# Cross-attention and expert feed-forward kernel: transposing the softmax probabilities with VectorE blocks and a round trip through DRAM instead of on TensorE

## The chip, the cores and the metric

One core of one Trainium2 chip runs the whole program. The metric is the device time of one execution in microseconds (us). TensorE is called PE, VectorE DVE, ScalarE ACT, GpSimd POOL and SyncE, which only issues transfers, SP.

## The reference

`x` and `ctx` are 128 batches of 64 rows by 128 features, float32. One layer of cross attention (16 heads of 64) and one expert feed-forward, each with a residual:

```python
x = x + xattn(ctx, layernorm(x), mask, ...)
    # kv_in = concat(norm(features), norm(latents))   128 rows: 64 of ctx, 64 of x
    # sim   = (lat @ Wq) (kv_in @ Wk)^T * scale, masked; alphas = softmax(sim)
    # out   = (alphas @ (kv_in @ Wv)) @ Wo
x = x + ffn(layernorm(x), ...)
    # 8 experts of width 64, the best 2 per row weighted by a sigmoid gate, and one shared expert of 128
```

## The kernel before

The weights are folded first: `MV[0]` holds Wq Wk^T per head and `MV[1]` Wv Wo per head, so that scores are (lat MV[0]) kv_in^T and the attention's result is the sum over heads of (alphas kv_in) MV[1]. Work goes in **frames**, `i` counts them: one frame is a group of 4 batches (`GB`), and there are 32 groups (`NG`). A frame has 8 steps, `k` = 0 to 7, and `e = 8 * i + k` numbers the steps of the program. In a step one **half** enters: 8 heads of one batch, that is four pairs of heads (`PAIRS`), 128 by 128 scores each. There are 256 halves.

A half `c` goes through these stages, each written in the step given here:

- PE, L858: four score products, float32, into PSUM bank `S_ps` (step c)
- DVE, L654: mask added and maximum taken, `logits` (step c+1)
- ACT, L531: four exponentials with their sums, `probs`, `denom` (step c+1)
- DVE, L662: `rdenom`, and POOL, L430: `probs` times `rdenom` (step c+2)
- PE, L838: four transposes of 128 by 128 by a product with the identity, into PSUM bank `PT_ps`; ACT, L504: `pT_hi`, the rounded high part; DVE, L687: `pT_lo`, what is left (step c+3)
- PE, L796 to L798 (`matmul3`): three products of high and low parts of `kv_in` and `pT` into `C_ps`; ACT, L510: `cT_hi`; DVE, L697: `cT_lo` (step c+4)

`MV[1]` is applied to `cT` of a whole group in the next frame, `W_ps`, heads spread over steps 0 to 5. Beside these stages each frame norms the keys of the group two frames on (POOL, with statistics by DVE at L738 and L743), transposes them (PE, L872), projects the queries of the next group (two heads a step, `T_ps`, copied by ACT to `tT`), adds the residual and takes statistics (DVE, L707 to L716), computes the gate (DVE, L579 to L617), and runs the feed-forward of the group before (PE into `H_ps`, ACT `h_tanh`, DVE `h_silu` and `h`, POOL `h` times `gates`, PE `Y_ps`).

There is no scheduler: each engine's instructions are written out by hand in the order of a loop over frames and steps, fully unrolled, and an engine starts an instruction only after all earlier ones of its own have started. `wait_ge` on a semaphore is the only other ordering. SP issues, once a frame: two loads `kv_raw`, one `mask_raw`, one `x_res`, four small stores to `gates_dram`, two loads `gates` and one store of `out`.

Of the kernel before, what the change touches and what calls it, by code (L numbers as in the profile page):

```python
# [5 lines left out]
def xattn_moe_ffn_kernel(nc, x, ctx, mask, ln_m_w, ln_m_b, ln_l_w, ln_l_b, Wq, Wk, Wv, Wo,  # L6
# [26 lines left out]
    with es:  # L33
# [3 lines left out]
        def sem(name):  # L37
            return es.enter_context(nc.semaphore(name))
# [25 lines left out]
        kv_hi = [sb(f"kv_hi{n}", [P, GB, D], f32r) for n in range(2)]  # L64
        kv_lo = [sb(f"kv_lo{n}", [P, GB, D], f32r) for n in range(2)]
# [43 lines left out]
        h = [sb(f"h{n}", [P, NT + 1, GT]) for n in range(2)]  # L109
# [3 lines left out]
        with ExitStack() as setup_only:  # L113
# [8 lines left out]
            su("unused", [P, 5 * H * DH])  # L122
            w13_stage = [su(f"w13_stage{n}", [P, (NT + 1) * P]) for n in range(2)]
        cT_hi = [sb(f"cT_hi{n}", [P, H, GB, S], f32r) for n in range(2)]
        cT_lo = [sb(f"cT_lo{n}", [P, H, GB, S], f32r) for n in range(2)]
# [3 lines left out]
        PT_ps, C_ps, T_ps, WY_ps, H_ps, X_ps = banks[1:7]  # L129
# [36 lines left out]
        pT_in_psum = sem("pT_in_psum")  # L166
        pT_hi_ready = sem("pT_hi_ready")
        pT_lo_ready = sem("pT_lo_ready")
        C_in_psum = sem("C_in_psum")
        cT_hi_ready = sem("cT_hi_ready")  # L170
        cT_lo_ready = sem("cT_lo_ready")
        W_in_psum = sem("W_in_psum")
# [54 lines left out]
        def has_half(j, p, k, lag):  # L227

            return has(j, p, 0, NG - 1) if k >= lag else has(j, p, 1, NG)

        def half_buffers(p, k, lag):

            return (k - lag) % HALVES, (p if k >= lag else 1 - p)

        def query_chunk(j, p, k):


            ahead = 1 if k >= 3 else 0
            return ((k + 5) % HALVES, ahead) if has(j, p, -ahead, NG - 1 - ahead) else None

        def query_chunk_before(j, p, k):

            if k == 0:
                return (4, 0) if has(j, p, 0, NG - 1) else None
            return query_chunk(j, p, k - 1)

# [24 lines left out]
        def last_bank(r, a=0):  # L271

            return (PT_ps, C_ps, T_ps, S_ps[1], X_ps)[NT if r == NT else 2 * (r % 2) + a]
# [16 lines left out]
        def _(sp):  # L290
# [30 lines left out]

            def frame(j, p):
                i = 2 * j + p
                if has(j, p, -1, NG - 3):
                    load_kv(j, p + 2)
                    load_mask(j, p + 2)
                if has(j, p, 0, NG - 1):

                    after(sp, x1_step, 3 * (i - 2) + 1)
                    sp.dma_start(x_res[p][:, :, :],  # L330
                                 x.rearrange("b s d -> (b s) d")[bass.ds(GT * i, GT), :].rearrange("(t q) d -> q t d", q=P)
                                 ).then_inc(x_res_loaded[p], 16)
                if has(j, p, 2, NG):

                    sp.wait_ge(gate_step, GATE_STEPS * (i - 1))
                    after(sp, gates_loaded, 32 * (i - 2))
                    for a in range(P // QUAD):
                        sp.dma_start(gates_dram.rearrange("e (t a q) -> e t a q", t=TT, a=P // QUAD)[:, :, a, :],
                                     g_denseT[QUAD * a:QUAD * a + E, :, :]).then_inc(gates_stored, 16)
                    sp.wait_ge(gates_stored, 64 * (i - 1))  # L340
                    after(sp, h_routed_done, NT * (i - 2))
                    for a in range(2):
                        sp.dma_start(gates[FH * a:FH * (a + 1), :, :],
# [13 lines left out]
        def _(pool):  # L357
# [64 lines left out]
            def frame(j, p):  # L422
                i = 2 * j + p
                for k in range(HALVES):
# [16 lines left out]
                    if k == 0 and has(j, p, 2, NG):  # L441
                        center(i - 1)
# [528 lines left out]
```

## Time and profile before

| | |
|---|---|
| median of 3 runs | 1170.12 us (1167.87 to 1170.26) |
| profiled execution, its own time | 1168.01 us |
| its span (first to last instruction in the trace) | 1166.3 us |
| instructions | 29786 |
| busy share of the span | PE 98%, DVE 78%, ACT 77%, POOL 57% |
| mean granted PE clock | 0.994 of full |
| DMA | 42.61 MB moved, SP's queue 12.9% of the 16 engines |

The span is cut into frames; from the fourth frame on each repeats the one before to the hundredth of a microsecond. A timeline row gives the start, the length and the instruction. Lengths on one engine can overlap, so what an instruction costs its engine is the distance from its start to the next start. For a row of SP the length is the time that SP is held by issuing the transfer, not the transfer.

### The profile page before, as it was taken

Reading aid. Unit: us, or ns where it says so; the run is one execution under the profiler, and the core shown is the slowest. Engines: PE = TensorE matmul, PEld = TensorE weight load, DVE = VectorE, ACT = ScalarE, POOL = GpSimd, SP = SyncE. Lnnn points to the kernel's source line nnn. Section 1 sums busy time; section 2 is a strip of 40 time slices with the busy share of each in tenths; the row PEclk is TensorE's granted clock in tenths of the full one; section 3 lists DMA queues with packets and bytes.
Section 4 is the critical chain, followed back from the end, with each engine's and each line's share of the span. In section 5 each row is a group of like instructions: output and inputs, shape, how many; then the busy total and the mean of one; then the engine's idle time right before and its main releaser. Section 6 shows DMA issues by size and latency. Waiting matters only on the chain.

```text
span 1166.3 us, 29786 instructions
## 1 busy us (share of the span) xinstructions
PE 1137.6 (98%) x9000; PEld 1091.1 (94%) x9000; DVE 908.2 (78%) x4095; ACT 901.8 (77%) x3180; POOL 669.5 (57%) x781
## 2 busy tenths in 40 slices
PE   5899999999999999999999999999999999999997
PEld 5899999999999999999999999999999999999986
DVE  3778787788787788787788787788787788887776
ACT  3988788777788777788777788777788777788771
POOL 5664656665656665656565656565656565656441
PEclk8999999999999999999999999999999999999998
DMA  6001001111001111001111001111001111001101
GB/s 160 24 11 38 20 24 42 42 42 42 20 24 42 43 42 42 21 24 42 43 42 42 21 24 42 43 42 42 21 24 42 43 43 40 22 24 29 29 24 33
DMA packets 64399, 42.61 MB, mean 37 GB/s; under 512 B 8944, under 2 KB 63856, under 8 KB 64240
## 3 DMA queue, kind: packets, MB, share of 16 engines
q1 hardware_dynamic: 63056, 39.66, 12.9%
q8 instruction: 73, 1.20, 0.4%
q10 hardware_dynamic: 1184, 1.05, 0.4%
q14 instruction: 86, 0.70, 0.2%
HBM read 36.25 MB, written 4.45 MB: 35 GB/s over the span
## 4 chain that ended last, share of the span: by engine, by line
PE 94%; DVE 2%; issue 1%; ACT 1%; POOL 1%; DMA 1%; POOLq 0%; SPq 0%; DVEq 0%; ACTq 0%
PE bank L858 19%; PE bank L796 19%; PE bank L798 18%; PE bank L797 18%; PE bank L838 9%; PE bank L802 6%; PE bank L872 2%; PE bank L920 1%; DMA wk_raw<-in_L_xattn_Wk 1%; PE bank L909 1%; PE bank L864 1%; PE bank L779 0%; DVE MV_lo L762 0%; DVE out_sb L632 0%; ACT probs L531 0%
## 5 line engine op out<-in xcount | busy, mean ns | idle before, releaser
L430 POOL TENSOR_TENSOR probs<-probs,rdenom 128x512 f32<-128x512 f32 x256 | 266.6, 1042 | 317.4 <-DVE rdenom L662 317.4
L531 ACT ACTIVATE probs<-logits,neg_max 128x128 f32<-128x128 f32 x1024 | 402.5, 413 | 0.5 <-DVE neg_max L654 0.5
L858 PEld LDWEIGHTS bank<-kvT,tT 128*128 128x128 f32 x2048 | 267.3, 191 | 22.5
L858 PE MATMUL bank<-kvT,tT 128*128 128x128 f32 x2048 | 269.3, 274 | 0.0
L654 DVE CUSTOM_DVE_ANT_0 logits<-bank,mask_add 128x128 f32<-128x128 f32 x1024 | 232.3, 282 | 5.4 <-PE bank L858 5.1
L687 DVE TENSOR_TENSOR pT_lo<-bank,pT_hi 128x512 fp32r<-128x512 f32 x256 | 175.2, 684 | 55.1 <-ACT pT_hi L504 47.2
L531 ACT ACTIVATION_READ_ACCUMULATOR probs<-logits,neg_max 128x1 f32 x1024 | 213.5, 208 | 0.0
L504 ACT CAST pT_hi<-bank 128x512 fp32r<-128x512 f32 x256 | 152.6, 596 | 47.7 <-PE bank L838 47.2
L491 ACT ACTIVATE h_tanh<-bank 128x256 f32<-128x256 f32 x160 | 61.5, 384 | 160.9 <-PE bank L798 159.0
L697 DVE TENSOR_TENSOR cT_lo<-bank,cT_hi 128x512 fp32r<-128x512 f32 x256 | 174.7, 683 | 0.3
L796 PE MATMUL bank<-latT_hi,MV_hi 128*128 128x256 f32 x512 | 166.6, 325 | 1.9 <-DVE latT_lo L726 1.5
L510 ACT CAST cT_hi<-bank 128x512 fp32r<-128x512 f32 x256 | 154.8, 605 | 8.7 <-PE bank L798 1.0
L838 PE MATMUL bank<-ident,probs 128*128 128x128 f32 x1024 | 154.1, 273 | 4.1 <-POOL probs L430 4.1
L498 ACT COPY tT<-bank 128x512 f32<-128x512 f32 x256 | 148.8, 581 | 5.2 <-PE bank L798 5.1
L798 PE MATMUL bank<-latT_hi,MV_lo 128*128 128x256 f32 x512 | 145.4, 284 | 0.0
L797 PE MATMUL bank<-latT_lo,MV_hi 128*128 128x256 f32 x512 | 144.2, 282 | 0.0
L796 PE MATMUL bank<-cT_hi,MV_hi 128*128 128x256 f32 x512 | 143.3, 280 | 0.2 <-DVE cT_lo L697 0.2
L797 PE MATMUL bank<-cT_lo,MV_hi 128*128 128x256 f32 x512 | 141.8, 277 | 0.0
L798 PE MATMUL bank<-cT_hi,MV_lo 128*128 128x256 f32 x512 | 141.7, 277 | 0.0
L838 PEld LDWEIGHTS bank<-ident,probs 128*128 128x128 f32 x1024 | 118.5, 141 | 5.6 <-POOL probs L430 5.5
L796 PE MATMUL bank<-pT_hi,kv_hi 128*128 128x512 f32 x256 | 122.2, 477 | 0.2
L675 DVE SCALAR_TENSOR_TENSOR h_silu<-h_tanh,bank 128x256 f32<-128x256 f32 x160 | 65.2, 408 | 51.7 <-ACT h_tanh L491 51.2
(111 smaller groups left out, 2615.4 us busy)
## 6 DMA issues: line engine op xcount, KB each, us to landing
gates<-gates_dram SPq DMA_DIRECT2D x62, 256.0 KB, 4.1
kv_raw<-in_ctx SPq DMA_DIRECT2D x32, 128.0 KB, 2.7
kv_raw<-in_x SPq DMA_DIRECT2D x32, 128.0 KB, 2.8
mask_raw<-in_mask_BxS_ik SPq DMA_DIRECT2D x32, 128.0 KB, 3.4
x_res<-in_x SPq DMA_DIRECT2D x32, 128.0 KB, 3.1
out<-out_sb SPq DMA_DIRECT2D x32, 128.0 KB, 1.8
gates_dram<-g_denseT SPq DMA_DIRECT2D x124, 2.0 KB
wv_raw<-in_L_xattn_Wv ACTq DMA_DIRECT2D x1, 512.0 KB, 5.3
```

What stands on the lines that cost most here:

```text
L430: nc.gpsimd.tensor_tensor(probs[n][:, :, :], probs[n][:, :, :], rdenom[n][:, :].unsqueeze(2).broadcast_to([P, PAIRS, P]), ALU.mult).then_i ...
L504: nc.scalar.copy(pT_hi[n][:, :], PT_ps[:, :]).then_inc(pT_hi_ready, 1)
L510: nc.scalar.copy(cT_hi[par][:, 8 * (kl // 4):8 * (kl // 4) + 8, kl % 4, :], C_ps[:, :].rearrange("p (h q) -> p h q", h=8)).then_inc(cT_hi_ ...
L531: nc.scalar.activation(probs[n % 4][:, r, :], logits[n % 2][:, r, :], ACT.Exp, bias=neg_max[n % 2][:, r:r + 1], scale=-1.0, accum_out=deno ...
L654: nc.vector.tensor_tensor_reduce(out=logits[kl % 2][:, r, :], in0=S_ps[(k - 1) % 2][:, P * r:P * (r + 1)], in1=mask_add[par][:, kl % 4, :] ...
L687: nc.vector.tensor_tensor(pT_lo[n][:, :], PT_ps[:, :], pT_hi[n][:, :].bitcast(fp32), ALU.subtract).then_inc(pT_lo_ready, 1)
L697: nc.vector.tensor_tensor(cT_lo[par][:, hs, kl % 4, :], C_ps[:, :].rearrange("p (h q) -> p h q", h=8), cT_hi[par][:, hs, kl % 4, :].bitcas ...
L796: nc.tensor.matmul(dst, w_hi, m_hi, start=first, stop=False)
L797: nc.tensor.matmul(dst, w_hi, m_lo, start=False, stop=False)
L798: return nc.tensor.matmul(dst, w_lo, m_hi, start=False, stop=last)
L838: last = nc.tensor.transpose(PT_ps[:, P * r:P * (r + 1)], probs[(k - 3) % 4][:, r, :], ident[:, :])
L858: last = nc.tensor.matmul(S_ps[k % 2][:, P * r:P * (r + 1)], tT[:, k % 4, hd:hd + 2, :], kvT[p][:, k % 4, :], start=True, stop=True)
```

## The change

Half `c` is now transposed in two moves. ACT writes `probs` as [128 rows, 4 column blocks, 4 pairs, 32], DVE transposes every 32 by 32 block in place of its block (`nc.vector.transpose`, one instruction of 128x512, into `probsT`), SP stores `probsT` to DRAM (256 KB) and SP loads it back with the blocks in their transposed places, by four loads of 64 KB, one for each 32 partitions, into `pT` in SBUF. The high part is cast from `pT` by ACT. The low part is made by DVE for even halves and by POOL for odd ones. The four PE transposes are gone and `C_ps` has two banks.

The steps are shifted: scores of half `c` are now written in step c-2, `logits` and exponentials in step c-1, `rdenom` and the POOL product in step c, the DVE transpose and the store in step c+1, the loads in step c+2, `pT_hi` and `pT_lo` in step c+3 and the value product in step c+4. `cT` is kept once and no longer twice; the projection of the group before reads it by a strided pattern (`head_columns`) and is guarded by `W_front_done`. `kv_hi` and `kv_lo` have three buffers. The key transposes and their casts move from step 2 to step 0, the keys' statistics from step 5 to step 2, and SP's once-a-frame transfers get places of their own: steps 0, 1, 5 and 6.

```diff
-        probs = [sb(f"probs{n}", [P, PAIRS, P]) for n in range(4)]
+        probs = [sb(f"probs{n}", [P, P // QUAD, PAIRS, QUAD]) for n in range(4)]
+        probsT = [sb(f"probsT{n}", [P, PAIRS * P]) for n in range(2)]
+        probsT_dram = [nc.dram_tensor(f"probsT_dram{n}", [P, PAIRS * P], fp32, kind="Internal").ap() for n in range(3)]
+        pT = [sb(f"pT{n}", [P, PAIRS * P]) for n in range(3)]
...
-        cT_hi = [sb(f"cT_hi{n}", [P, H, GB, S], f32r) for n in range(2)]
+        cT_hi = sb("cT_hi", [P, GB, 2, PAIRS * P], f32r)
...
@@ SP @@
+            def store_probs(s):
+                n = s % 3
+                sp.wait_ge(probsT_ready, s + 1)
+                after(sp, pT_loaded[n], 64 * (s // 3))
+                sp.dma_start(probsT_dram[n], probsT[s % 2][:, :]).then_inc(probsT_stored[n], 16)
+
+            def load_probs(s):
+                n = s % 3
+                sp.wait_ge(probsT_stored[n], 16 * (s // 3 + 1))
+                if s >= 3:
+                    sp.wait_ge(pT_lo_ready[(s - 3) % 2], (s - 3) // 2 + 1)
+                for c in range(P // QUAD):
+                    sp.dma_start(pT[n][QUAD * c:QUAD * (c + 1), :].rearrange("k (a f) -> k a f", a=P // QUAD),
+                                 probsT_dram[n].rearrange("(a k) (c f) -> c k a f", a=P // QUAD, c=P // QUAD)[c]
+                                 ).then_inc(pT_loaded[n], 16)
...
+                for k in range(HALVES):
+                    e = HALVES * i + k
+                    if has_half(e - 1):
+                        store_probs(e - 1)
+                    if has_half(e - 2):
+                        load_probs(e - 2)
+                    if k == 0 and has(j, p, -1, NG - 3):
+                        load_kv(j, p + 2)
+                        load_mask(j, p + 2)
...
@@ ACT, step e @@
+                    if has_half(e - 3):
+                        c = e - 3
+                        act.wait_ge(pT_loaded[c % 3], 64 * (c // 3 + 1))
+                        after(act, C_in_psum, c - 1)
+                        nc.scalar.copy(pT_hi[c % 2][:, :], pT[c % 3][:, :]).then_inc(pT_hi_ready, 1)
...
+                    if has_half(e + 1):
+                        c = e + 1
+                        for r in range(PAIRS):
+                            act.wait_ge(logits_ready, PAIRS * c + r + 1)
...
@@ DVE, step e @@
+                    if has_half(e):
+                        n = e % 4
+                        dve.wait_ge(exp_done, PAIRS * (e + 1))
...
                         nc.vector.reciprocal(rdenom[n][:, :], denom[n][:, :]).then_inc(rdenom_ready, 1)
+                    if has_half(e - 1):
+                        c = e - 1
+                        dve.wait_ge(probs_ready, c + 1)
...
+                        nc.vector.transpose(probsT[c % 2][:, :], probs[c % 4][:, :, :, :].rearrange("p c r k -> p (c r k)")
+                                            ).then_inc(probsT_ready, 1)
...
@@ POOL, step e @@
+                    if has_half(e - 3) and (e - 3) % 2 == 1:
+                        c = e - 3
+                        pool.wait_ge(pT_hi_ready, c + 1)
+                        after(pool, C_in_psum, c - 1)
+                        nc.gpsimd.tensor_tensor(pT_lo[1][:, :], pT[c % 3][:, :], pT_hi[1][:, :].bitcast(fp32),
+                                                ALU.subtract).then_inc(pT_lo_ready[1], 1)
...
@@ PE, step e @@
-                        for r in range(PAIRS):
-                            last = nc.tensor.transpose(PT_ps[:, P * r:P * (r + 1)], probs[(k - 3) % 4][:, r, :], ident[:, :])
-                        last.then_inc(pT_in_psum, 1)
```

SP's queue before, one whole frame, from the store of `out` to the loads of `gates` (numbers behind names are buffers, a row with x3 stands for three equal ones, and brackets hold the semaphores that a row waits for):

```order
L348 DMA out_0<-out_sb1 128x2x128 [waits out_ready]
L294 DMA kv_raw1<-in_ctx_1024 64x4x128 [waits kv_step]
L296 DMA kv_raw1<-in_x 64x4x128
L302 DMA mask_raw1<-in_mask_BxS2_ik0 128x256 [waits mask_ready]
L330 DMA x_res1<-in_x 128x2x128 [waits x1_step]
L338 DMA gates_dram<-g_denseT 16x1x32 [waits gates_loaded,gate_step]
L338 DMA gates_dram<-g_denseT 16x1x32 x3
L343 DMA gates<-gates_dram 64x4x256 [waits h_routed_done,gates_stored]
L343 DMA gates<-gates_dram 64x4x256
```

SP's queue now, first the gate stores of step 5 and the half's transfers of step 6, then step 0 of the next frame; L335 is the store of a half and L343 its four loads:

```order
L371 DMA gates_dram<-g_denseT 16x1x32 [waits gates_loaded,gate_step]
L371 DMA gates_dram<-g_denseT 16x1x32 x3
L335 DMA probsT_dram1<-probsT1 128x512 [waits pT_loaded1,probsT_ready]
L343 DMA pT0<-probsT_dram0 32x4x128 [waits pT_lo_pool_ready,probsT_stored0]
L343 DMA pT0<-probsT_dram0 32x4x128 x3
...
L335 DMA probsT_dram0<-probsT1 128x512 [waits pT_loaded0,probsT_ready]
L343 DMA pT2<-probsT_dram2 32x4x128 [waits pT_lo_pool_ready,probsT_stored2]
L343 DMA pT2<-probsT_dram2 32x4x128 x3
L303 DMA kv_raw0<-in_ctx_1024 64x4x128 [waits kv_step]
L305 DMA kv_raw0<-in_x 64x4x128
L311 DMA mask_raw0<-in_mask_BxS2_ik0 128x256 [waits mask_ready]
L386 DMA out_0<-out_sb0 128x2x128 [waits out_ready]
```

Every step now has a store and four loads, the store of half e-1 stands ahead of the loads of half e-2, and the old transfers stand between them.

DVE before, step 5 of a frame:

```order
L662 RECIPROCAL rdenom3<-denom3 128x4 [waits probs_ready,exp_done]
L675 SCALAR_TENSOR_TENSOR h_silu<-h_tanh,bank5 128x256 [waits h_prod_done,tanh_done]
L679 TENSOR_TENSOR h0<-h_silu,bank5 128x256 [waits y_in_psum,silu_done]
L687 TENSOR_TENSOR pT_lo0<-bank1,pT_hi0 128x512 [waits C_in_psum,pT_hi_ready]
L697 TENSOR_TENSOR cT_lo0<-bank2,cT_hi0 128x8x64 [waits cT_hi_ready]
L738 BN_STATS kv_bn<-kv_raw0 128x6 [waits kv_mv_done,kv_loaded0]
L738 BN_STATS kv_bn<-kv_raw0 128x6 x3
L743 BN_AGGR kv_mv<-kv_bn 128x2 [waits kv_step,kv_bn_done]
L743 BN_AGGR kv_mv<-kv_bn 128x2 x3
L654 ISA logits1,neg_max1<-bank7,mask_add0 128x128 [waits exp_done,S_in_psum]
```

DVE now, the same feed-forward tile's place, step 6 into step 7:

```order
L711 RECIPROCAL rdenom2<-denom2 128x4 [waits probs_ready,exp_done]
L717 STREAM_TRANSPOSE probsT1<-probs1 128x512 [waits probsT_stored0,probs_ready]
L731 SCALAR_TENSOR_TENSOR h_silu<-h_tanh,bank5 128x256 [waits h_prod_done,tanh_done]
L735 TENSOR_TENSOR h1<-h_silu,bank5 128x256 [waits y_in_psum,silu_done]
L755 TENSOR_TENSOR cT_lo<-bank1,cT_hi 128x512 [waits cT_hi_ready]
L702 ISA logits0,neg_max0<-bank0,mask_add0 128x128 [waits exp_done,mask_ready,S_in_psum]
L702 ISA neg_max0 128x1
...
L711 RECIPROCAL rdenom3<-denom3 128x4 [waits probs_ready,exp_done]
L717 STREAM_TRANSPOSE probsT0<-probs2 128x512 [waits probsT_stored1,probs_ready]
L722 TENSOR_TENSOR out_sb0<-bank4,x1_0 128x256 [waits out_stored0,y_in_psum]
L745 TENSOR_TENSOR pT_lo0<-pT1,pT_hi0 128x512 [waits C_in_psum,pT_hi_ready]
L755 TENSOR_TENSOR cT_lo<-bank2,cT_hi 128x512 [waits cT_hi_ready]
```

The block transpose stands behind the reciprocal of the half after it: `probs2` is transposed behind the reciprocal of `denom3`.

ACT before, step 6:

```order
L498 COPY tT<-bank3 128x2x4x64 [waits S_in_psum,t_in_psum]
L504 CAST pT_hi1<-bank1 128x512 [waits C_in_psum,pT_in_psum]
L510 CAST cT_hi1<-bank2 128x8x64 [waits C_in_psum]
L478 COPY attnT<-bank4 128x256 [waits attn_in_psum,W_in_psum]
L531 ACTIVATE probs1,denom1<-logits1,neg_max1 128x128 [waits pT_in_psum,logits_ready]
L531 ACTIVATE probs1,denom1<-logits1,neg_max1 128x128 [waits logits_ready] x3
```

ACT now, step 6:

```order
L543 COPY tT<-bank3 128x2x4x64 [waits S_in_psum,t_in_psum]
L549 CAST pT_hi1<-pT2 128x512 [waits C_in_psum,pT_loaded2]
L558 CAST cT_hi<-bank1 128x512 [waits C_in_psum]
L523 COPY attnT<-bank4 128x256 [waits attn_in_psum,W_in_psum]
L588 ACTIVATE probs3,denom3<-logits1,neg_max1 128x4x32 [waits probsT_ready,logits_ready]
L588 ACTIVATE probs3,denom3<-logits1,neg_max1 128x4x32 [waits logits_ready] x3
```

The four exponentials of half e+1 (`probs3`) stand behind `pT_hi` of half e-3 (`pT2`), which waits for its loads.

## Rows read from the trace of the kernel before

**Rows 1.** The page: busy time of the engines; chain that ended last.

```profile
PE 1137.6 (98%) x9000; PEld 1091.1 (94%) x9000; DVE 908.2 (78%) x4095; ACT 901.8 (77%) x3180; POOL 669.5 (57%) x781
...
PE 94%; DVE 2%; issue 1%; ACT 1%; POOL 1%; DMA 1%; POOLq 0%; SPq 0%; DVEq 0%; ACTq 0%
```

**Rows 2.** One frame in windows: length, busy PE, PEld, DVE, ACT, POOL; clock; DMA.

```profile
601.66:636.70 35.04, 34.96 (x279) 33.67 (x279) 27.91 (x127) 27.87 (x100) 20.90 (x24) 1.00 0.13 36
```

**Rows 3.** Timeline of PE in one step: start, length, instruction (us).

```profile
603.32 0.60 PE L838 MATMUL bank<-ident,probs 128*128 128x128 f32 x4
603.67 0.48 PE L796 MATMUL bank<-pT_hi,kv_hi 128*128 128x512 f32 x1
603.99 0.40 PE L797 MATMUL bank<-pT_lo,kv_hi 128*128 128x512 f32 x1
604.23 0.39 PE L798 MATMUL bank<-pT_hi,kv_lo 128*128 128x512 f32 x1
```

**Rows 4.** Timeline of ACT in one step: two casts, then the exponentials.

```profile
604.41 0.58 ACT L504 CAST pT_hi<-bank 128x512 fp32r<-128x512 f32 x1
604.88 0.59 ACT L510 CAST cT_hi<-bank 128x512 fp32r<-128x512 f32 x1
...
606.83 0.20 ACT L531 ACTIVATION_READ_ACCUMULATOR probs<-logits,neg_max 128x1 f32 x1
```

**Rows 5.** Timeline of DVE in one step.

```profile
605.17 0.66 DVE L687 TENSOR_TENSOR pT_lo<-bank,pT_hi 128x512 fp32r<-128x512 f32 x1
605.75 0.68 DVE L697 TENSOR_TENSOR cT_lo<-bank,cT_hi 128x512 fp32r<-128x512 f32 x1
606.35 0.28 DVE L654 CUSTOM_DVE_ANT_0 logits<-bank,mask_add 128x128 f32<-128x128 f32 x1
...
607.19 0.17 DVE L662 RECIPROCAL rdenom<-denom 128x4 f32<-128x4 f32 x1
```

**Rows 6.** Timeline of DVE: the pieces that only some steps have.

```profile
603.13 0.41 DVE L707 TENSOR_TENSOR x<-bank,x_res 128x256 f32<-128x256 f32 x1
...
604.10 0.25 DVE L716 BATCH_NORM_AGGREGATE x_mv<-x_bn 128x2 f32<-128x6 f32 x2
...
624.79 0.25 DVE L617 STREAM_TRANSPOSE g_denseT<-g_dense 128x64 f32<-128x64 f32 x1
...
628.37 0.86 DVE L738 BATCH_NORM_STATS2 kv_bn<-kv_raw 128x6 f32<-128x128 f32 x4
629.26 0.38 DVE L743 BATCH_NORM_AGGREGATE kv_mv<-kv_bn 128x2 f32<-128x6 f32 x4
```

**Rows 7.** Groups of instructions by line: count, busy, mean ns.

```profile
L408 POOL TENSOR_TENSOR kv_lo<-kv_f,kv_hi 128x512 fp32r<-128x512 f32 x32 | 41.2, 1288 | 0.1
...
L587 DVE TENSOR_TENSOR g_eq<-g_score 128x128 f32<-128x128 f32 x32 | 24.6, 769 | 0.0
...
L585 DVE TENSOR_TENSOR g_gt<-g_score 128x128 f32<-128x128 f32 x32 | 14.7, 459 | 0.0
```

**Rows 8.** Timeline of SP's queue: start, time to issue, transfer.

```profile
625.06 2.89 SPq L338 DMA_DIRECT2D gates_dram<-g_denseT  x4
...
636.26 0.39 SPq L348 DMA_DIRECT2D out<-out_sb  x1
636.70 0.61 SPq L294 DMA_DIRECT2D kv_raw<-in_ctx  x1
...
638.00 0.60 SPq L302 DMA_DIRECT2D mask_raw<-in_mask_BxS_ik  x1
```

**Rows 9.** The page, DMA issues: KB each, then us from issue to landing.

```profile
kv_raw<-in_ctx SPq DMA_DIRECT2D x32, 128.0 KB, 2.7
```

**Rows 10.** Landing of the x_res loads, L330: min, median, max.

```profile
DMA to landing us min/median/max: 2.0/3.1/4.5
```

**Rows 11.** Windows with the granted clock behind the busy times.

```profile
22.00:24.00 2.00, 1.03 (x5) 1.04 (x6) 1.48 (x7) 0.38 (x2) 0.00 (x0) 0.50 0.00 0
```

**Rows 12.** First and last start of the score matmuls' weight loads.

```profile
L858 PEld LDWEIGHTS bank<-kvT,tT x2048: 186/192/192, 28.6 to 1124.7; 128*128 128x128 f32 x187
```

More of the change, by code:

```diff
@@ L63, in xattn_moe_ffn_kernel @@
         kv_f = sb("kv_f", [P, GB, D])
-        kv_hi = [sb(f"kv_hi{n}", [P, GB, D], f32r) for n in range(2)]
-        kv_lo = [sb(f"kv_lo{n}", [P, GB, D], f32r) for n in range(2)]
+        kv_hi = [sb(f"kv_hi{n}", [P, GB, D], f32r) for n in range(3)]
+        kv_lo = [sb(f"kv_lo{n}", [P, GB, D], f32r) for n in range(3)]
         kvT = [sb(f"kvT{n}", [P, GB, P]) for n in range(2)]
@@ L322, in frame @@
             def frame(j, p):
                 i = 2 * j + p
[L324 to L343, printed above, removed]
-                                     gates_dram.rearrange("(r a) t -> a r t", a=2)[a, :, :].partition_broadcast(FH)
-                                     ).then_inc(gates_loaded, 16)
@@ L351, in _, with store_out @@
+                if i == NG + 2:
+                    store_out(i)
+            def store_out(i):
+                after(sp, out_ready, i - 2)
+                sp.dma_start(out.rearrange("b s d -> (b s) d")[bass.ds(GT * (i - 3), GT), :].rearrange("(t q) d -> q t d", q=P),
+                             out_sb[(i - 1) % 2][:, :, :]).then_inc(out_stored[(i - 1) % 2], 16)
             frames(sp, frame)
@@ L722, in frame @@
                                                 ALU.subtract).then_inc(x2T_lo_ready, 1)
-                    if k == 2 and has(j, p, -1, NG - 2):
+                    if k == 0 and has(j, p, -1, NG - 2):
                         dve.wait_ge(latT_hi_ready, i + 2)
@@ L732, in frame @@
                         gate_part({3: 7, 4: 12}[k])
-                    if k == 5 and has(j, p, -2, NG - 3):
+                    if k == 2 and has(j, p, -2, NG - 3):
                         dve.wait_ge(kv_loaded[p], 32 * (j + 2))
@@ L850, in frame @@
-                    if has_half(j, p, k, 0):
-                        if k == 0:
-                            pe.wait_ge(kvT_ready, i + 1)
-                        if k in (0, 4):
-                            pe.wait_ge(t_ready, e + 4)
-                        after(pe, logits_ready, PAIRS * (e - 1))
-                        for r in range(PAIRS):
-                            hd = 8 * (k // 4) + 2 * r
-                            last = nc.tensor.matmul(S_ps[k % 2][:, P * r:P * (r + 1)], tT[:, k % 4, hd:hd + 2, :],
-                                                    kvT[p][:, k % 4, :], start=True, stop=True)
+                    if has_half(e - 4):
+                        c = e - 4
+                        g, kl = c // HALVES, c % HALVES
+                        pe.wait_ge(pT_lo_ready[c % 2], c // 2 + 1)
+                        if kl == 0:
+                            pe.wait_ge(kv_step, KV_STEPS * (g + 1))
+                        after(pe, cT_lo_ready, c - 1)
+                        matmul3(C_ps[c % 2][:, :], kv_hi[g % 3][:, kl % 4, :], kv_lo[g % 3][:, kl % 4, :],
+                                pT_hi[c % 2][:, :], pT_lo[c % 2][:, :]).then_inc(C_in_psum, 1)
@@ new lines, in frame @@
+                    if has_half(e + 2):
+                        c = e + 2
+                        g, kl = c // HALVES, c % HALVES
+                        if kl == 0:
+                            pe.wait_ge(kvT_ready, g + 1)
+                        if kl in (0, 4):
+                            pe.wait_ge(t_ready, c + 4)
+                        after(pe, logits_ready, PAIRS * (c - 1))
+                        for r in range(PAIRS):
+                            hd = 8 * (kl // 4) + 2 * r
+                            last = nc.tensor.matmul(S_ps[c % 2][:, P * r:P * (r + 1)], tT[:, kl % 4, hd:hd + 2, :],
+                                                    kvT[g % 2][:, kl % 4, :], start=True, stop=True)
```

201 lines of the change are left out of this document (106 added, 95 removed).

## The prediction

> **What bounds the kernel now.** I read the page first: PE is busy for 98% of the span, and the chain that ended last is 94% PE [rows 1]. Then one frame of the steady part in windows: 35.04 us long, PE busy in 34.96 of it, DVE in 27.91, ACT in 27.87, POOL in 20.90 [rows 2]. So PE sets the pace and nothing stops it; the others have 7 us or more to spare in a frame. What leaves PE is gained, up to the point where another engine, or a ring of waits, is slower than the rest of PE's work. That point has to be found.
>
> **What PE gains.** The four transposes start at 603.32 and the value product behind them at 603.67: 0.35 us a step, not the 0.60 of their row, since they overlap. The first value product also holds PE from 603.67 to 603.99, 0.32 us, where the next, of equal size, takes 0.24 [rows 3]. I count that 0.08, the change from float32 transposes to rounded operands, as gained too. 0.43 us a step, 3.5 a frame: PE would need 31.5 us, and 256 halves would give back 110 us. The strided read of `cT` in the projection I cost at nothing, as its runs are 32 elements; at the worst it is hidden if PE is no longer the bound.
>
> **What the others get.** The block transpose is one instruction of 512 columns; the trace has one of 64 columns, 0.25 us [rows 6]. A cast or subtraction of 512 columns takes 0.68 there [rows 5]. Between one element at the cost of the difference, (0.68 - 0.25) / 448, and a slower form I take 0.71; the ends are 0.6 and twice the column time, 1.2. DVE loses half of its `pT_lo`, 4 a frame at 0.68: 27.9 + 8 x 0.71 - 4 x 0.68 = 30.9 us a frame. POOL gets 4 `pT_lo` with two full operands, 1.29 each as for `kv_lo` [rows 7]: 20.9 + 5.2 = 26.1. ACT keeps its work. All are under 31.5, DVE narrowly. As sums of work this change would pay.
>
> SP gets one store and four loads a step. A DMA that covers all partitions with flat rows holds SP 0.39 us; `kv_raw`, whose 3-D form (64x4x128) is nearest to the new loads (32x4x128), holds it 0.61, and starts follow each other by 0.65 (636.70 to 638.00 for two); the small gate stores take 0.72 each (four in 2.89) [rows 8]. I take 0.43 for the store and 0.65 for a load (ends 0.45 and 0.72): 3.03 us a step. Beside that, a frame has 2.93 in step 5 (gate stores), about 1.3 in step 6 (gate loads), and 2.4 in step 0 (`kv_raw` twice, `mask_raw`, `out`): 24.2 + 7 = 31.3 us. SP alone would be as long as PE.
>
> **The ring of waits.** This is the step on which my forecast rests. SP issues the store of half c, which waits for its transpose, ahead of the loads of half c-1. The transpose of c stands on DVE behind the reciprocal of c+1, which waits for the exponentials of c+1. Those stand on ACT behind `pT_hi` of half c-3, which waits for its loads. So the loads of c-3 release, two steps later, the loads of c-1: a ring that must turn once in two steps. Its length, from the start of `pT_hi`:
>
> - to the end of the last exponential's sum: 604.41 to 607.03, 2.62 us [rows 4]
> - reciprocal, and the next instruction 0.1 behind it, with a semaphore: 0.2
> - block transpose: 0.71, in all 3.53
> - store issued: 0.43, to 3.96; three loads ahead of the last: 1.95, to 5.91
> - last load, issue to landing: `kv_raw` takes 2.7 for 128 KB [rows 9], the fastest `x_res` 2.0 [rows 10]. These are 64 KB: 2.3, to 8.2
>
> That is 8.25 us with semaphores for two steps, where PE needs 7.9 on average. With loads issued at 0.47 and landing in 2.0 it is 7.4; with 0.72 and 2.7 it is 8.9.
>
> On top come pieces that stand inside the ring in some steps. On DVE, between `cT_lo` and the next reciprocal: in step 7 the residual and its statistics, 603.13 to 604.35, less a little overlap, 1.15; in step 2 the keys' statistics, 628.37 to 629.64, 1.25 with a slack of 0.1 there, 1.15 [rows 6]. With `pT_lo` 0.58, `cT_lo` 0.60 and `logits` 0.84 [rows 5] DVE's own way from `pT_hi` to the reciprocal is as long as ACT's, so they add in full. In step 4 small gate instructions add 0.25.
>
> SP adds in-order work where its queue is longer: 3.03 + 2.93 = 5.96 us in step 5 and 3.03 + 2.4 = 5.4 in step 0. The longest way through a frame takes SP through step 5 (5.96), the ring over steps 6 and 7 (8.25 + 1.15), SP through step 0 (5.4), the ring over steps 1 and 2 (8.25 + 1.15), the ring over steps 3 and 4 (8.25 + 0.25): **38.7 us a frame** against 35.04. With the short ends it is 34.7, with the long ones 41.
>
> **The sum.** The first score product starts at 28.6 and the last at 1124.7 [rows 12]; 29 frames of 35.04 end there, so that the first three take about 80 us. They hold less (no feed-forward yet), and I give the ring 3.7 less in two of them: 3 x 38.7 - 7.4 = 109 for 80. The stages now reach over six steps from scores to value product where they reached over four: 8 us once. The profiled execution took 1168.01 us for a span of 1166.3, 2 us below the median of 1170.12, which is inside the spread. So time = 1168 + 29 (F - 35.04) + (3F - 7.4 - 80) + 8 = 72 + 32 F, F being the frame. F = 38.7 gives **1310 us**. No change would need F = 34.2.
>
> The Trainium skill, "DMA: Bandwidth & Descriptors", Rules for kernel authors, speaks against the new form as well: transfers under 64 KB are mostly overhead and small ones should be joined. Its fit for one transfer issued by GpSimd, 2.0 us and the bytes at 436 GB/s, gives an estimate of 2.15 for a load of 64 KB; the ring would be 8.1 us by it and the time about 1296, by three turns a frame. The rows above (2.0 to 2.7) agree with it in size; no row here shows a transfer of this shape.
>
> **Rivals.**
>
> - The ring turns faster than I think and PE stays the bound: F = 31.5, and since the first frames are not slower either, 1168 - 110 + 8 = 1066 us. For it: no engine's sum of work is over 31. Against: even the short ends give 34.7. It decides if the ring is under 6.9 us. 0.08.
> - The short ends hold (issue 0.47, landing 2.0): F = 34.7, 1182 us, and a little less would be faster. 0.14, half of it on each side of no change.
> - DVE becomes the bound. `pT_lo` on DVE now reads two operands from SBUF. `g_gt` and `g_eq` are twins in form, yet take 459 and 769 ns [rows 7], and `g_eq` is the one that runs while POOL works. If each `pT_lo` waits out half of a POOL instruction (0.6), and the transpose costs 1.2, DVE has 30.9 + 4 x 0.6 + 8 x 0.5 = 37.3 us: 1266 us with no ring at all. 0.06.
>
>   The Trainium skill, "SBUF — State Buffer", SBUF: two separate sides, has the rule: a DVE instruction with two SBUF inputs and a GpSimd instruction lock each other out for a whole instruction. The trace agrees: `g_eq` is 310 ns longer than its twin.
> - PE, which will wait inside each frame, is granted the lower of its two clocks. From 22 to 24 us, after a stop, the granted clock was 0.50, that is 1.2 GHz [rows 11]. Products of 256 columns then stand 0.21 apart and not 0.12; PE would need 31.5 x 1.75 = 55 us a frame, 1830 us. Against it: my waits are under 2 us each and PE stays busy 80%. 0.04.
>
> The ring with F from 36 to 41.5 keeps 0.68.
>
> **How the numbers follow.** The likeliest case gives 1310 us, its own range 1220 to 1400. To hold 8 in 10 the range has to take in most of the short-ends case: 1170 to 1400. Measurement can tell about 0.2% from no change, 2 us. Faster: 0.08 and 0.07 and 0.01, 0.16. Same 0.03. Slower 0.81.
>
> **What would show it.** Right: ACT's largest idle time is before `pT_hi`, ended by the DMA that writes `pT`; the chain that ended last is made of ACT, DVE, SP and DMA and PE is a small part; PE busy 80%; steady frames of 37 to 41 us, with the longest gaps around SP's steps 5 and 0; the loads issue in 0.6 to 0.65 us. Wrong: loads that hold SP 0.4 us or land in under 2 us; frames of 31.5 us with PE still at 98%; DVE busy over 95%, with transposes above 1 us; a granted clock well under 1. The prediction fails as a whole if the transposed halves land before ACT has come to them, because then no ring exists and the 110 us of PE are a plain gain.

## The result and the profile after

The changed kernel takes **1324.05 us** (median of 4 runs, 1318.99 to 1329.88) against 1168.99 (4 runs) for the kernel before on the same chip: 1.133 times as long, interval 1.129 to 1.137. I forecast 1310. The profiled execution took 1329.88 us for a span of 1327.9. One run of the ninth experiment was over 1.5% slower than the fastest of its kernel and is left out of its numbers.

The page of the changed kernel: span, busy time of the engines, and the chain that ended last, which is followed back from the last instruction through whatever released each step. PE had 98% and 94% of the chain in [rows 1].

```profile
span 1327.9 us, 29870 instructions
PE 1119.5 (84%) x7976; PEld 1033.0 (78%) x7976; DVE 1039.4 (78%) x4223; ACT 914.0 (69%) x3180; POOL 859.2 (65%) x909
DVE 30%; SPq 20%; issue 12%; DMA 11%; PE 11%; ACT 9%; POOL 6%; DVEq 0%; ACTq 0%; POOLq 0%
```

No engine is the bound: the chain runs through all of them. Two frames in windows, and 5 us inside the first of them (length, busy PE, PEld, DVE, ACT, POOL, granted clock, DMA share, GB/s); they answer to [rows 2]:

```profile
602.13:641.17 39.04, 34.70 (x248) 31.95 (x248) 32.24 (x132) 28.61 (x102) 27.22 (x29) 0.96 0.47 139
641.17:680.23 39.06, 34.54 (x246) 32.08 (x246) 31.19 (x131) 27.73 (x99) 26.64 (x29) 0.96 0.46 140
612.00:617.00 5.00, 3.12 (x12) 2.83 (x13) 3.81 (x14) 4.40 (x15) 3.61 (x4) 0.66 0.54 164
```

A frame is 39.05 us here (39.2 as a mean over 30 frames, from the gate stores at 124.9 and 1302) and was 35.04. The waits, in total, times and longest:

```profile
POOL probs L469 <- DVE rdenom L711: 293.2, 189, 3.8
ACT pT_hi L549 <- DMA pT<-probsT_dram: 248.4, 166, 4.0
PE bank L854 <- POOL pT_lo L486: 96.9, 44, 4.2
PE bank L854 <- DVE pT_lo L745: 54.9, 63, 3.2
```

ACT waits for the loaded block two steps in three, and PE waits 152 us for low parts, 97 of it for those of POOL. How long the trip is: SP's time for a load (min, median, max in ns), and the page's rows of store and load (KB each, median us to landing), where [rows 8] and [rows 9] gave the nearest forms:

```profile
L343 SPq DMA_DIRECT2D pT<-probsT_dram x1024: 302/432/2270, 38.4 to 1289.3; - x171
probsT_dram<-probsT SPq DMA_DIRECT2D x256, 256.0 KB, 2.1
pT<-probsT_dram SPq DMA_DIRECT2D x1024, 64.0 KB, 2.1
```

The chain through one frame, in order of time (start, length, what):

```profile
635.82 0.34 SPq L335
...
638.18 0.72 SPq L371
...
641.17 0.38 SPq L335
...
643.05 2.00 DMA pT<-probsT_dram
645.07 0.63 ACT pT_hi L549
...
648.27 0.28 POOL x_ve L496
...
649.32 1.01 POOL probs L469
650.34 0.57 POOL x L453
...
651.60 1.23 POOL pT_lo L486
652.87 0.50 PE bank L854
...
659.39 0.43 ACT tT L543
...
662.62 0.28 DVE kv_mv L801 x3
...
674.89 0.34 SPq L335
```

Read as sections: SP without a gap through steps 5 and 6 (store, four loads, four gate stores, store, four loads), 635.82 to 643.05, 7.23 us; the last load lands, 2.02; ACT and DVE, 3.20; POOL, from x1's variance through the rescale and the centring to the low part, 4.60; PE, 6.52; ACT, 3.23; DVE through steps 2 to 5, 12.27. The sum is 39.07. In such a stretch one frame earlier DVE (third busy time) was busy for 4.93 of 5 us:

```profile
625.00:630.00 5.00, 4.07 (x32) 3.73 (x31) 4.93 (x17) 3.73 (x14) 4.20 (x5) 1.00 0.33 105
```

PE's timeline where the low part comes (the bracket is idle time and who ended it):

```profile
613.88 0.79 PE L854 MATMUL bank<-pT_hi,kv_hi 128*128 128x512 f32 x1 [2.67 <-POOL pT_lo L486]
614.47 0.63 PE L855 MATMUL bank<-pT_lo,kv_hi 128*128 128x512 f32 x1
614.90 0.63 PE L856 MATMUL bank<-pT_hi,kv_lo 128*128 128x512 f32 x1
```

After 2.67 us without work the products of 512 columns start 0.43 apart, where they stood 0.24 apart in [rows 3]; the mean granted clock of those 5 us is 0.66, that is partly the lower level of 1.2 GHz. The stop comes once a frame, the slow stretch in most frames: of 30 stretches of a frame's length, 9 have a granted clock of 1.00, and behind the stop of 2.77 us that ends at 219.26 the products of 512 columns stand 0.23 apart. In the frame of the chain above the slow stretch starts a little later: the products of 512 columns stand 0.23 apart there and those of 256 columns, 655.44 to 657.57, 0.21 instead of 0.12. So a part of PE's 6.52 us in the chain is the lower clock.

### The profile page after: what moved, and what is told of

It is laid out like the page before. It is cut to its first block, busy times and chain, and to the rows that moved or that the text cites. A ratio compares the mean times of both kernels' runs of the same rounds, so it can differ in the third digit from the quotient of the medians.

```text
span 1327.9 us, 29870 instructions
## 1 busy us (share of the span) xinstructions
PE 1119.5 (84%) x7976; PEld 1033.0 (78%) x7976; DVE 1039.4 (78%) x4223; ACT 914.0 (69%) x3180; POOL 859.2 (65%) x909
## 4 chain that ended last, share of the span: by engine, by line
DVE 30%; SPq 20%; issue 12%; DMA 11%; PE 11%; ACT 9%; POOL 6%; DVEq 0%; ACTq 0%; POOLq 0%
SPq L343 11%; DMA pT<-probsT_dram 11%; SPq L371 5%; DVE probsT L717 5%; ACT probs L588 4%; DVE logits L702 4%; DVE cT_lo L755 3%; PE bank L854 3%; SPq L335 2%; PE bank L912 2%; PE bank L855 2%; PE bank L856 2%; POOL pT_lo L486 2%; DVE h L735 2%; ACT pT_hi L549 2%
## 5 line engine op out<-in xcount | busy, mean ns | idle before, releaser
L549 ACT CAST pT_hi<-pT 128x512 fp32r<-128x512 f32 x256 | 159.4, 623 | 249.1 <-DMA pT<-probsT_dram 248.4
L912 PEld LDWEIGHTS bank<-kvT,tT 128*128 128x128 f32 x2048 | 284.3, 201 | 23.8 <-issue 0.2
L912 PE MATMUL bank<-kvT,tT 128*128 128x128 f32 x2048 | 286.0, 285 | 0.1
L854 PE MATMUL bank<-pT_hi,kv_hi 128*128 128x512 f32 x256 | 123.5, 482 | 152.4 <-POOL pT_lo L486 96.9
L588 ACT ACTIVATION_READ_ACCUMULATOR probs<-logits,neg_max 128x1 f32 x1024 | 201.3, 197 | 0.0
L854 PEld LDWEIGHTS bank<-pT_hi,kv_hi 128*128 128x128 f32 x256 | 49.3, 193 | 179.5 <-POOL pT_lo L486 107.0
L486 POOL TENSOR_TENSOR pT_lo<-pT,pT_hi 128x512 fp32r<-128x512 f32 x128 | 163.7, 1279 | 27.8 <-ACT pT_hi L549 27.4
L717 DVE STREAM_TRANSPOSE probsT<-probs 128x512 f32<-128x512 f32 x256 | 175.6, 686 | 0.5 <-issue 0.5
L745 DVE TENSOR_TENSOR pT_lo<-pT,pT_hi 128x512 fp32r<-128x512 f32 x128 | 108.6, 849 | 67.0 <-ACT pT_hi L549 66.9
L558 ACT CAST cT_hi<-bank 128x512 fp32r<-128x512 f32 x256 | 149.8, 585 | 1.3 <-PE bank L856 1.2
L855 PE MATMUL bank<-cT_lo,MV_hi 128*128 128x256 f32 x512 | 147.2, 288 | 0.0
```

The costliest lines, as they stand in the source:

```text
L486: nc.gpsimd.tensor_tensor(pT_lo[1][:, :], pT[c % 3][:, :], pT_hi[1][:, :].bitcast(fp32), ALU.subtract).then_inc(pT_lo_ready[1], 1)
L549: nc.scalar.copy(pT_hi[c % 2][:, :], pT[c % 3][:, :]).then_inc(pT_hi_ready, 1)
L558: nc.scalar.copy(cT_hi[:, kl % 4, kl // 4, :], C_ps[c % 2][:, :]).then_inc(cT_hi_ready, 1)
L588: nc.scalar.activation(probs[c % 4][:, :, r, :], logits[c % 2][:, r, :].rearrange("p (c k) -> p c k", k=QUAD), ACT.Exp, bias=neg_max[c % 2 ...
L717: nc.vector.transpose(probsT[c % 2][:, :], probs[c % 4][:, :, :, :].rearrange("p c r k -> p (c r k)")).then_inc(probsT_ready, 1)
L854: nc.tensor.matmul(dst, w_hi, m_hi, start=first, stop=False)
```

## The experiments

Times are medians; ratios are to the kernel before, with the 95% interval. The changed kernel has 1.133. The theory at the start was the prediction's ring of waits (the loads of one half release, through ACT, DVE and SP, the loads two steps later); its rival was that POOL's low part holds PE.

**1. The block transpose ahead of the reciprocal.** This takes away the ring's link "the transpose of c stands behind the reciprocal of c+1".

```
+                    if has_half(e - 1):
...
+                        nc.vector.transpose(probsT[c % 2][:, :], ...
                     if has_half(e):
...
                         nc.vector.reciprocal(rdenom[n][:, :], denom[n][:, :])...
-                    if has_half(e - 1):
...
-                        nc.vector.transpose(probsT[c % 2][:, :], ...
```

> The changed kernel with one edit on DVE: the block transpose of half e-1 stands at the head of step e, ahead of the logits of e+1 and of the reciprocal of half e, for which it has no need. Ring theory (the wait for the loads turns once in two steps because the transpose is queued behind the next half's reciprocal): the ring now has three steps for some 8.5 us, is slower than PE nowhere, and the frame falls from 39.05 us to 32 to 35, the time to 1100 to 1190 us. Rival, POOL (the low parts given to POOL, and the low PE clock after the wait for them, are the cost): the time stays within 2% of the changed kernel, above 1297. Rival, SP's queue as such is full: the same, above 1297.

The edit puts the transpose ahead of the reciprocal, but not ahead of the logits of e+1, as I had written; those wait for exponentials of two steps before and do not close the ring.

Measured: 1335.33, 1.142 [1.139, 1.145]. Not faster, even slightly slower. With one of its links cut, the ring of two steps would have been some microseconds shorter; it did not set the pace. The edit also lengthens another way: POOL's rescale waits for the reciprocal, which now stands behind the transpose. From `pT_hi` to PE's start behind POOL's low part the chain takes 8.24 us (649.13 to 657.37) where it took 7.80 (645.07 to 652.87), and PE's wait for POOL's low part grew from 96.9 to 116.6 us. In 32 frames that would be about 14 us, an estimate; the loss is 11.

**2. SP issues the loads first.**

```
- if has_half(e - 1): store_probs(e - 1)
  if has_half(e - 2): load_probs(e - 2)
+ if has_half(e - 1): store_probs(e - 1)
```

> The changed kernel with one edit on SP: in each step the loads of half e-2 are issued ahead of the store of half e-1. Ring theory: the loads no longer wait for the next half's transpose, the ring spans three steps, but SP now stands still until the store has landed (2.1 us) and then issues 1.9 us of loads, 4.0 a step, 34 a frame with its other transfers: 34 to 36 us a frame, 1160 to 1230 us. Rival, POOL: no change, above 1297. Rival, a full SP queue: slower than the changed kernel, since SP waits more.

Measured: 1282.12, 1.098 [1.095, 1.100]: 42 us gained, between the two expectations. SP's order counts, but it is not the whole.

**3. No trip through DRAM.** VectorE transposes straight into the tile that ScalarE reads. This leaves out the exchange of the 32 by 32 blocks, so the value product takes partly transposed probabilities.

```
- store_probs(e - 1); load_probs(e - 2)
- nc.vector.transpose(probsT[c % 2] ...)   + nc.vector.transpose(pT[c % 3] ...)
```

> The changed kernel without the round trip through DRAM: DVE transposes into pT, and ACT casts from there. It leaves out the exchange of the 32 by 32 blocks, so the value product takes partly transposed probabilities. All else stays: the transposes on DVE, the low parts on DVE and POOL, one cT. Ring theory: frame 31.5 to 34 us, 1080 to 1150 us, set by PE and DVE. Rival, POOL: above 1270, as its low parts and the wait of PE for them are still there.

Measured: 1231.11, 1.054 [1.052, 1.056]. The trip costs 93 of the 155 us; the other 62 stay without it. The result lies between the two expectations, so neither theory was enough alone.

**4. The kernel before with one of its four PE transposes** (the others are left out, so three quarters of the value product's input are stale).

```
- for r in range(PAIRS):
+ for r in range(PAIRS if e == 3 else 1):
```

> The kernel before with one PE transpose a half in place of four (from the second half on; it leaves out three quarters of the transposes, so the value product takes stale probabilities). It sizes what PE gains. If a transpose costs its start-to-start share, 0.35 / 4 = 0.0875 us: 3 x 256 x 0.0875 = 67 us less, about 1102 us. If it costs what the page's busy time says (0.15 each): 115 us less, 1054. If PE was not the bound: no change.

Measured: 1123.74, 0.962 [0.960, 0.963]: 45 us, 0.059 a transpose, not 0.0875, between the expectations of 1102 and of no change. PE's busy time fell by 70 us (1137.6 to 1067.4), and 25 came back as waits. The first value product in it, with the idle time ahead:

```profile
L796 PE MATMUL bank<-pT_hi,kv_hi 128*128 128x512 f32 x256 | 121.8, 476 | 15.2 <-DVE cT_lo L697 15.1
```

That wait is for DVE; another 12.2 us stand ahead of the keys' transposes, ended by ACT's `g_exp`. With a little less work PE already meets DVE and ACT. The engines behind PE were nearer than their busy shares said.

**5 to 8. Four edits of the changed kernel.** The new theory P was the chain as shown above: POOL's low part stops PE once a frame, and the low clock adds to it.

```
5: - if has_half(e - 3) and (e - 3) % 2 == 1: ... nc.gpsimd.tensor_tensor(pT_lo[1] ...)
   - if has_half(e - 3) and (e - 3) % 2 == 0:   + if has_half(e - 3): (VectorE)
6: 3 and 5 together
7: POOL's low part moved up, to behind the rescale of the probabilities
8: - if k == 5: for a in range(4): store of the gates
   + if k in (5, 6): for a in (0, 1) if k == 5 else (2, 3); loads at k == 7
```

> The changed kernel with every low part by VectorE; GpSimd has none. Theory P (the frame's low part on GpSimd, behind x1's statistics, rescale and centring, stops TensorE 2.3 to 2.7 us once a frame, and the low clock behind it costs 2 to 3 us more): VectorE gets 4 x 0.7 us a frame, GpSimd loses 4 x 1.28, TensorE's waits for GpSimd's low part (96.9 us) are gone, and the time is 1230 to 1280. Rival R (the round trip through DRAM sets the frame, and GpSimd's wait only lies beside it): 1310 to 1345. Rival D (VectorE, 32 us of a 39 us frame, becomes the bound): above 1345.

> No store and load of the probabilities (VectorE transposes straight into the tile that ScalarE reads, so the exchange of blocks between quadrants is left out), and every low part by VectorE. With the low parts split this took 1231. Theory P: another 40 to 90 us go, 1140 to 1190. Rival D (VectorE is the bound once nothing else waits: some 31.5 us + 2.8 of low parts, less the stretching by GpSimd, and its dependences): 1200 to 1250.

> The changed kernel with GpSimd's low part put straight behind its rescale of the probabilities in each step, ahead of the centring of x1 and the products of h. Theory P: in step 0 two passes over x1 (2 x some 0.9 us) no longer stand ahead of the low part that TensorE waits for, so most of the wait of 2.7 us a frame goes, and the clock's loss with it: 1240 to 1290. Rival R: 1310 to 1340. The centring comes 1.3 us later in its place; if that makes TensorE wait for the transposes of x2 instead, the time is also as before the edit.

> The changed kernel with the four stores of the gates two in step 5 and two in step 6, and the gates' loads in step 7. Theory S (SP's steps 5 to 6 are on the path of each frame, its queue there 5.35 us long): 1.4 to 3 us a frame go, 1230 to 1280. Rival (the round trips are short there and what is late is late by VectorE's 12 us without a gap in steps 2 to 5, to which SP's work in step 5 only adds): 1300 to 1330, no change beyond 1%.

Measured: 5, 1326.97, 1.135 [1.132, 1.138]. 6, 1215.13, 1.040 [1.039, 1.042]. 7, 1318.85, 1.130 [1.128, 1.132]. 8, 1301.44, 1.113 [1.112, 1.115].

Theory P as the only cause falls by run 5: with POOL's low part gone, the time is the same. Run 7 says less, since its edit does not take the stop away: PE waits 82.8 us for POOL's low part (96.9 before). Its timeline shows what keeps the low part late:

```profile
609.86 0.62 ACT L549 CAST pT_hi<-pT 128x512 fp32r<-128x512 f32 x1 [2.44 <-DMA pT<-probsT_dram]
611.88 0.79 PE L854 MATMUL bank<-pT_hi,kv_hi 128*128 128x512 f32 x1 [2.44 <-POOL pT_lo L476]
```

POOL is free 1.00 us before the high part comes, and starts the low part at 610.55; the loads are late at the same place. What stands there in run 5, its chain shows, in the stretch in which POOL and PE stood before. After the last transpose of step 0 it now goes through SP:

```profile
646.59 0.34 SPq L335
...
648.88 0.62 SPq L303
...
650.20 0.60 SPq L311
650.85 0.43 SPq L386
651.38 0.41 SPq L335
...
653.39 3.87 DMA pT<-probsT_dram
657.28 0.63 ACT pT_hi L543
```

Store, loads, the two `kv_raw` loads, mask, output, store, loads: 6.8 us of issue, and then a landing of 3.87 instead of 2.0; `kv_raw` and mask are in flight at that time. That two ways of nearly equal length lie side by side in steps 0 and 1, one through POOL and PE and one through SP and DMA, so that taking one away shows the other, is read from the chains of runs 5 and 7. SP's steps 5 and 6 are in both, and run 8, which thins them, gains 23 us; that is 0.7 a frame, half of the least that its theory S expected (1.4).

Run 6 shows the other limit. Its page, and one instruction of its DVE timeline:

```profile
PE 1079.9 (89%) x7976; PEld 997.4 (82%) x7976; DVE 1146.4 (94%) x4351; ACT 909.8 (75%) x3180; POOL 730.9 (60%) x781
625.01 1.62 DVE L735 TENSOR_TENSOR pT_lo<-pT,pT_hi 128x512 fp32r<-128x512 f32 x1
```

Without the trip and with all low parts on it, DVE is busy for 94%: 1215 is about its own bound. Theory P had 1140 to 1190 here.

**9 to 12. The trip taken apart.**

```
9:  8, and load_mask and store_out moved from k == 0 to k == 3
10: 9 and 2 together
11: 3 without the block transpose (a constant tile is read, the probabilities are not used)
12: - nc.scalar.copy(pT_hi[c % 2], pT[c % 3])   + nc.scalar.copy(pT_hi[c % 2], probsT[c % 3])
    (the low parts too, and three buffers of probsT; stores and loads go on as before,
    but their data are not used, and the loads no longer wait for the low parts)
```

> The changed kernel with the gates' stores two and two in steps 5 and 6, their loads in step 7, and the mask's load and the output's store moved from step 0 to step 3, where SP waits for VectorE. Splitting the gates alone gave 23 us. Theory S (SP's queue between two steps is on the path twice a frame, in steps 5 to 6 and in steps 0 to 1): the mask and output issues (0.60 + 0.43 us and their gaps, 1.1 us a frame) come off as well, 35 us, so 1260 to 1275. Rival L (step 1's loads land late anyway, by the kv load's bytes, or other work holds step 1): no more than the 23 us, 1295 to 1305.

> The kernel before this one with the loads of step e-2's block issued ahead of the store of e-1's as well. The two edits alone gave 23 us and 42 us. Theory S: they take different stretches off the same path, so they add up or more: 1215 to 1245, near the 1231 of the kernel without any trip. Rival: they shorten the same stretch, 1260 to 1285.

> No trip through DRAM and no block transpose either: ScalarE and the low parts read a constant tile, so the probabilities are computed but not used in the value product. With VectorE's transposes and no trip it was 1231. Theory V (VectorE's 8 transposes of 0.6 to 0.7 us a frame and what they hold up carry the 1231 above TensorE's bound of about 1100 to 1124): 1120 to 1170. Rival G (GpSimd's low part behind x1's chain holds TensorE once a frame whatever VectorE does): 1190 to 1230.

> The changed kernel with every store and load of the probabilities issued and moved as before, but into a tile that nobody reads: ScalarE and the low parts read VectorE's transposed tile (three buffers of it, the exchange of blocks is left out). Theory L (the trip costs by its length, in issue and landing, on the waiting path): 1225 to 1245, as without the trip. Rival C (its 134 MB slow the other transfers and the engines by contention): above 1270.

Measured: 9, 1280.68 (three runs, 1278.27 to 1292.46), 1.099 [1.093, 1.105]. 10, 1248.12, 1.069 [1.066, 1.071]. 11, 1217.33, 1.042 [1.040, 1.044]. 12, 1230.23, 1.053 [1.051, 1.055].

Run 12 moves all the bytes and costs as much as the kernel without them (run 3, 1231.11). Its GB/s by slices are at the changed kernel's level (133 in the mean there, 144 here):

```profile
GB/s 144 136 173 146 136 153 152 151 154 138 130 161 147 158 145 143 130 162 147 161 143 139 128 158 160 157 134 137 140 159 159 151 132 141 144 159 146 148 135 31
```

So the trip's 94 us are its length on the way that is waited for; rival C, contention, falls. Runs 8, 9 and 10 then take 76 us of it back by the order in SP's queue alone, step by step 23, about 20 and about 33. The edits nearly add up: loads first gave 42 alone, and run 10 came out 3 us above its expected 1215 to 1245. ACT's wait for the loads in run 10, where it was 248.4, and PE's for POOL:

```profile
PE bank L856 <- POOL pT_lo L488: 80.8, 38, 3.8
ACT pT_hi L551 <- DMA pT<-probsT_dram: 59.7, 50, 4.8
```

Run 9 gained 21 over run 8 by the medians and 17 by the ratios, where theory S expected 26 to 41 and its rival none: the way through SP in steps 0 to 1 counts, for less than I thought. Its runs scatter by 14 us, so the size is uncertain.

Run 11 was meant to show whether DVE's transposes carry the rest. They carry 14 us (1231 to 1217); rival G, POOL's low part, fits with 1190 to 1230. PE's largest idle time in it:

```profile
L844 PE MATMUL bank<-pT_hi,kv_hi 128*128 128x512 f32 x256 | 114.8, 448 | 107.7 <-POOL pT_lo L483 86.4 <-DVE pT_lo L735 21.3
```

And its chain, over a step without a stop and then over the stop:

```profile
619.63 0.89 PE bank L902 x8
...
624.22 1.04 DVE pT_lo L735
...
627.60 0.28 POOL x_ve L493
...
630.88 1.28 POOL pT_lo L483
632.21 0.50 PE bank L844
632.70 0.23 PE bank L845
632.93 0.23 PE bank L846
633.16 1.71 PE bank L902 x8
```

Five instructions of POOL and its low part, 4.6 us, stand between DVE's statistics and PE. Behind the stop the eight score products take 1.71 instead of 0.89, and the first value product 0.50 instead of 0.26. The second is not the clock: it takes 0.50 behind a wait of 0.39 us too (646.48 in the changed kernel). That POOL's low part is worth the rest is argued from this idle time. No run without trip and transposes moves it elsewhere, and the one that takes it from POOL without the trip (run 6) meets DVE's bound.

No kernel of the changed form beats the kernel before. The best version that leaves nothing out is run 10, 7% slower; even with the trip's waits away (runs 3, 6, 12) it is 4 to 5% slower.

## Why the prediction came out as it did

The direction and the size were right: 1310 for 1324, F = 38.7 for 39.2, and 72 + 32 F with F = 39.2 gives 1326. But the frame's parts were others than mine, and errors offset each other: that the total came within 1.1% is in good part luck. The signs that I had listed for "right" came true but for the issue time of the loads: ACT's largest idle time was before `pT_hi`, PE was 11% of the chain and 84% busy, frames took 39. They fit any long way through the same engines and could not tell it from the ring.

- **PE's gain** (110 us): about right as work, too large as time. Run 4 takes away three of four transposes: by 0.0875 each that is 67 us, and PE's busy time fell by 70, but the time only by 45, as waits took 25 back. I had counted what leaves PE as gained. It did not reach the result, since PE was no bound. The 0.08 for the first value product was not tested.
- **Sums of work**: the transpose 0.686 for 0.71; POOL's `pT_lo` 1.28 for 1.29; DVE 31.2 to 32.2 for 30.9; POOL 27 for 26.1. Right. DVE's excess is its stretched instructions (below).
- **SP's issue and the landing**: mis-sized. A load holds SP 0.43 us (median) and starts follow by 0.43 to 0.50, 0.47 in the mean, not 0.65; the store 0.34 (median), not 0.43; the median landing is 2.1, not 2.3. These are the short ends, and for these I had worked out F = 34.7 and 1182 us. They held, and the frame was 39 all the same: the sum of ring and queue is the step that failed as I put it. By my own list they even speak for "wrong".
- **The ring**: wrong as formulated. Run 1 cuts its link through the reciprocal and gains nothing; run 2 cuts its other link, SP's order, and gains 42. What stood in its place, by the chain, is a longer way once around the frame: two stretches of SP's queue (steps 5 to 6, and 0 to 1), with 12.3 us of DVE work in a row between them in steps 2 to 5. I had counted steps 1 to 4 as two turns of ring, 9.4 + 8.5.
- **SP's queue in steps 5 and 0**: the mechanism was right. The gate stores there were priced at 2.93 and are 2.9 long (638.18 to 641.17 is 2.99). Splitting them, moving mask and output, and issuing loads first is worth 76 us.
- **Missing altogether**: the low part on POOL behind x1's statistics. I gave POOL 26.1 us of 31.5 and took that as cover. It is a sum; at one place in the frame the low part has five POOL instructions ahead of it, while PE waits 2.3 to 2.7 us. In run 11 PE's idle time ahead of the value product is 107.7 us, 86.4 of it for POOL's low part and 21.3 for DVE's. 1124 less a fourth transpose at run 4's rate is 1109, and 1217 less 1109 is 108. The two numbers agree, which makes the account likely and does not show it: the lower clock behind the stop comes on top, and the changed kernel differs in more than that (the attention values lie otherwise, for one).
- **Rivals**: PE as the bound (1066) did not come. DVE as the bound (1266, from a price of 1.2 for the transpose and blocked `pT_lo`) is true of run 6 alone, at 1215 and by the stretched `pT_lo` (1.06 us). Its ground was in part misread: `g_eq` is not the only one of the twins beside POOL, which works from 617.63 to 620.17 in the kernel before, while `g_gt` starts at 618.34 and `g_eq` at 618.74. So the 310 ns between them do not measure the lock; better rows stand below. The low clock came, in a small part only: 0.96 as the mean, never 55 us a frame.

In one line: 1169 before; 1124 with three of four PE transposes gone; 1217 for the changed form with neither transpose nor trip; 1231 with the block transposes; 1230 with the bytes moved as well; 1324 when ACT waits for them. The last step, the trip, is shown by runs 3 and 12; what lies between 1124 and 1217 is the part that is argued.

## What to carry to other kernels

Work taken from the bound engine pays only if no step's chain through the other engines gets longer than the step. So trace what stands ahead of the new instruction on its own engine at its worst place in the frame; a sum of 27 us of 39 says nothing on it. This round trip through memory cost by its length on a waited-for way and its place in an in-order queue (94 us, of which reordering gave back 76), and not by its bytes (1230 against 1231 us): ask what else that queue issues just then. And a forecast that hits by its total proves none of its terms. When an edit of the named culprit changes nothing, first look whether the wait is gone at all, as it was not in run 7, and then read the new chain for a second way of the same length.

## What the runs showed of the hardware

- **DVE stretched by POOL.** The groups of two small DVE instructions, first of the kernel before, then of the changed one:

```profile
L602 DVE SCALAR_TENSOR_TENSOR g_keep<-g_rank,g_score 128x16 f32<-128x16 f32 x32 | 4.5, 140 | 0.1
L612 DVE TENSOR_TENSOR g_dense<-g_keep,g_rsum 128x16 f32<-128x16 f32 x32 | 5.4, 168 | 0.1
```

```profile
L649 DVE SCALAR_TENSOR_TENSOR g_keep<-g_rank,g_score 128x16 f32<-128x16 f32 x32 | 19.1, 596 | 0.1
L659 DVE TENSOR_TENSOR g_dense<-g_keep,g_rsum 128x16 f32<-128x16 f32 x32 | 19.1, 596 | 0.1
L745 DVE TENSOR_TENSOR pT_lo<-pT,pT_hi 128x512 fp32r<-128x512 f32 x128 | 108.6, 849 | 67.0 <-ACT pT_hi L549 66.9
```

  Instructions of 16 columns grew from 0.14 and 0.17 to 0.60 us as they came beside POOL's: `g_keep` starts at 670.21 and `g_dense` at 672.42, within POOL's instructions of 669.76 to 670.80 and 672.00 to 673.05, where POOL was idle at both in the kernel before. In run 5 `g_dense` meets an idle POOL (630.42) and is back at 0.17; `g_keep` still meets a busy one and stays at 0.60. `pT_lo` grew from 0.68 with one operand in PSUM to 0.85 with both in SBUF, 1.06 in run 6, up to 1.62. The rule of the Trainium skill, "SBUF — State Buffer", SBUF: two separate sides, that a VectorE instruction with two SBUF inputs and one of GpSimd that reads SBUF shut each other out whole, agrees with these rows.
- **Landing.** 64 KB in 128 rows of 512 bytes land 2.1 us after issue in the median (1.9 at the least, 4.6 at the most); the estimate from "DMA: Bandwidth & Descriptors" of the Trainium skill, 2.15 in the prediction, agrees. The 256 KB store lands in 2.1 too, where the same fit would give an estimate of 2.6: there the measurement differs, and size hardly counts between these two. With 384 KB of other loads and a 128 KB store issued just ahead it was 3.9.
- **The clock.** Around the stop of 2.67 us that ends at 613.88 the granted clock was 0.66 over 5 us, and the products behind it came at about half pace; behind the one of 2.77 us that ends at 219.26 it stayed at 1.00 (219 to 225). By the chain the value product and the scores took 3.19 us there (0.79, 0.43, 0.43, 1.54) and in run 11 2.67, against 1.61 without a stop: 1 to 1.6 us in a frame with a slow stretch, an estimate in which 0.24 is the longer first product, which is not the clock. In run 5, where PE's longest stop in the frame below is 1.32 us, the clock of that frame was 1.00 (windows, columns as above). One such frame proves little, as the changed kernel has some too; over the four runs the mean clock was 0.970 to 0.982 in run 5 and 0.959 to 0.961 in the changed kernel:

```profile
601.45:641.67 40.22, 34.45 (x253) 31.21 (x251) 34.95 (x135) 28.23 (x99) 22.30 (x25) 1.00 0.46 135
```
